# A two-layer recurrent kernel, second layer: gate products written straight to the token banks, scan carries copied by VectorE, a three-pass softplus, and a new order of jobs

## The reference

```python
xz = einsum('bld,ed->bel', xn, W_in);  x, z = split(xz, 2)         # 512 channels each
xc = silu(conv1d_causal(x, conv_w, K=4) + conv_b)
dt, Bm, Cm = split(einsum('bdl,ed->ble', xc, W_x), [128, 144])
delta = softplus(einsum('blr,dr->bdl', dt, W_dt) + b_dt)
state = exp(delta * A) * state + (delta * xc) * B_t                # 16 states a channel, a scan over time
y = sum over the states of C_t * state, + D * xc
y = y * silu(z)
s = einsum('bdl,ed->ble', y, W_out) + b_out
x = x + s * silu(xn @ binarized(weight).T + bias)
```

## Time and profile before

| | |
|---|---|
| median of 3 runs | 1458.35 us (1455.82 to 1458.52) |
| the profiled execution | 1456.31 us, of which the span 1454.5 us |
| busy over the span | PE 95%, DVE 71%, ACT 61%, POOL 62% |
| first scan of the second block to the last | 630.7 us to 1436.8 us |

### The profile page before, as it was taken

The page is one execution under the profiler, slowest core; times in us unless marked ns, Lnnn a source line. Parts: engine busy times, 40 slices in busy tenths (PEclk is TensorE's granted clock), DMA queues, the critical chain, the costliest instruction groups (busy, mean ns, idle before and its releaser), DMA issues.

```text
span 1454.5 us, 23554 instructions
## 1 busy us (share of the span) xinstructions
PE 1379.5 (95%) x8652; PEld 1076.8 (74%) x8652; DVE 1026.0 (71%) x1377; ACT 889.0 (61%) x1461; POOL 904.2 (62%) x578
## 2 busy tenths in 40 slices
PE   7999999999999999988899999999999999999887
PEld 4445469999999999456667767777767768768777
DVE  7755542332322323589899998999999998998996
ACT  4211121111111111399999989999999999999893
POOL 4222211232222222159989989989999989999995
PEclk9999999999999999989999999999999999999999
DMA  9921146766766764123342452533534443523532
GB/s 299 404 91 40 58 136 227 269 251 233 267 248 249 273 241 151 41 55 79 88 102 74 98 119 61 131 88 94 125 80 96 102 102 88 129 76 84 134 91 69
DMA packets 57761, 205.17 MB, mean 141 GB/s; under 512 B 6575, under 2 KB 32815, under 8 KB 48822
## 3 DMA queue, kind: packets, MB, share of 16 engines
q1 hardware_dynamic: 42358, 146.55, 28.9%
q0 software_dynamic: 15296, 57.19, 17.3%
HBM read 141.78 MB, written 31.00 MB: 119 GB/s over the span
## 4 chain that ended last, share of the span: by engine, by line
PE 49%; POOL 21%; DVE 10%; ACT 10%; issue 7%; DMA 3%; SPq 0%; POOLq 0%; DVEq 0%; ACTq 0%
PE bank L1518 17%; POOL hst L690 16%; PE bank L1531 8%; PE bank L1463 7%; DVE hst L1363 5%; ACT dA L883 4%; PE bank L1723 3%; PE bank L1703 3%; POOL dbuT L672 3%; ACT dbuT L872 2%; DMA hst<-hst 2%; PE bank L1585 2%; POOL xpad L650 1%; PE bank L1493 1%; PE bank L1592 1%
## 5 line engine op out<-in xcount | busy, mean ns | idle before, releaser
L1363 DVE TENSOR_TENSOR_SCAN hst<-dA,carry,bank 128x512 f32<-128x512 f32 x512 | 631.4, 1266 | 52.4 <-PE bank L1703 41.2
L690 POOL TENSOR_TENSOR hst<-hst,c_bc 128x2048 f32<-128x2048 f32 x127 | 581.8, 4592 | 20.9 <-DVE hst L1363 6.0
L1703 PEld LDWEIGHTS bank<-ident,dbuT 128*128 128x128 f32 x2048 | 241.7, 142 | 180.1 <-issue 93.0
L883 ACT ACTIVATE dA<-delta,negA 128x512 f32<-128x512 f32 x512 | 357.2, 714 | 5.9 <-DVE hst L1363 5.8
L1703 PE MATMUL bank<-ident,dbuT 128*128 128x128 f32 x2048 | 316.3, 278 | 41.0 <-DVE hst L1363 35.9
L872 ACT ACTIVATE dbuT<-duT,bT 128x512 f32<-128x512 f32 x382 | 271.8, 712 | 8.1 <-PE bank L1703 8.0
L1518 PEld LDWEIGHTS bank<-f_sb,w_gu 128*128 128x128 f32 x2240 | 255.5, 192 | 2.7 <-ACT f_sb L754 1.0
L1518 PE MATMUL bank<-f_sb,w_gu 128*128 128x128 f32 x2240 | 256.0, 275 | 0.7 <-ACT f_sb L754 0.7
L1723 PE MATMUL bank<-ident,hst 128*128 128x128 f32 x1520 | 215.7, 273 | 3.4 <-DMA hst<-hst 3.4
L625 POOL TENSOR_TENSOR x_sb<-x_sb,neg_half 128x1 f32<-128x1 f32 x35 | 23.0, 656 | 260.5 <-DVE x_sb L1180 260.5
L1723 PEld LDWEIGHTS bank<-ident,hst 128*128 128x128 f32 x1520 | 176.2, 142 | 4.2 <-DMA hst<-hst 4.1
(11 more groups left out here) (212 smaller groups left out, 1760.6 us busy)
## 6 DMA issues: line engine op xcount, KB each, us to landing
w_gu<-in_w_gu SPq DMA_DIRECT2D x35, 2048.0 KB, 7.3
c_bc<-c_rows SPq DMA_DIRECT2D x64, 512.0 KB, 4.2
hst<-hst POOLq DMA_DIRECT2D x31, 1024.0 KB, 9.1
sorted_x<-sg_a SPq DMA_DIRECT2D x12, 387.0 KB, 11.4
x_sb<-sorted_x SPq DMA_DIRECT2D x35, 129.0 KB, 7.2
x_sb<-in_x SPq DMA_DIRECT2D x8, 512.0 KB, 7.7
w_d<-in_w_d SPq DMA_DIRECT2D x1, 4096.0 KB, 21.3
x_mix<-x_sb SPq DMA_DIRECT2D x1, 4096.0 KB, 31.5
```

The costliest lines, as they stand in the source:

```text
L690: pool.tensor_tensor(h[:], h[:], c, ALU.mult).then_inc(hc_ready, 1)
L883: act.activation(dA[:, at % DA_BUFS, :], delta[q % B][:, d, :], ACT.Exp, scale=negA[:, d, n:n + 1]).then_inc(dA_ready, 1)
L1363: v.tensor_tensor_scan(h[:, d, :], dA[:, at % DA_BUFS, :], bank[4 + u % 2][:], carry1[q % B][:, n, d:d + 1], ALU.mult, ALU.add).then_inc(s ...
L1703: ins = pe.transpose(bank[4 + u % 2][:, i * P:(i + 1) * P], dbuT[(DS * q + n) % DBU_BUFS][:, i, d * P:(d + 1) * P], ident[:])
```

## The change

1. z: the products now run in the chunk that uses them, in units 9 to 14, and write to the token banks 0 to 3, each as soon as `gate_y` of the chunk before has read the bank. ScalarE applies silu while it reads the banks (four 128x512 instructions in unit 21), writes `zy`, and `add_skip` follows in units 18 and 19, waiting for that silu. VectorE's four copies are gone.
2. Carries: VectorE copies them (`keep_carry`), one 128x4 copy a state, after the first scan of the next state (`CARRY_AT`). GpSimd's multiply waits for that copy.
3. Softplus is max(v, ln(1 + exp(16) * exp(-max(16 - v, 0)))): three ScalarE passes, and one `scalar_tensor_tensor` on VectorE with the bias and the maximum.
4. The tables are rewritten: silu in units 21 and 22 rather than 24, two of GpSimd's four `dbuT` states moved (4, 7, 10, 11 to 4, 8, 9, 11), the sums given units one by one, du transposes and others some units earlier.

```diff
-POOL_SPREADS = (4, 7, 10, 11)
+POOL_SPREADS = (4, 8, 9, 11)
...
-                        pool.tensor_copy(carry1[q % B][:, n, :], h[:, :, CH - 1]).then_inc(carry_done, 1)
+                        pool.wait_ge(carry_done, g + 1)
                     pool.wait_ge(c_loaded[n // 2 % 2], 64 * q + 16 * (n // 4 + 1))
-                    if q < CHUNKS - B:
-                        pool.wait_ge(carry_done, g + 1)
...
-            def silu_z(t):
-                wait_freed(act, t - 1, "Z3")
-                act.activation(zy[t % B][:], zy[t % B][:], ACT.Silu).then_inc(z_ready, 1)
+            def silu_z(t, i):
+                act.wait_ge(z_made, TPC * t + i + 1)
+                act.activation(zy[t % B][:, i, :], bank[i][:], ACT.Silu).then_inc(z_ready, 1)
...
+            def below_cap(t, d):
+                wait_full(act, t, f"DL{d}")
+                act.activation(soft[:, d, :], place(t, f"DL{d}")[:], ACT.Relu, bias=cap_dt[:, d:d + 1],
+                               scale=-1.0).then_inc(soft_step, 1)
...
-                is_freed(v.tensor_tensor(delta[(t + 1) % B][:, d, :], place(t, f"DL{d}")[:], soft[:, d, :], ALU.add),
-                         t, f"DL{d}")
+                is_freed(v.scalar_tensor_tensor(delta[(t + 1) % B][:, d, :], place(t, f"DL{d}")[:],
+                                                cols1[:, d, KC + 1:KC + 2], soft[:, d, :], ALU.add, ALU.max), t, f"DL{d}")
...
+            def keep_carry(g):
+                q, n = divmod(g, DS)
+                v.wait_ge(scan_done, DB * g + DB)
+                v.tensor_copy(carry1[q % B][:, n, :], hst[g % STATE_BUFS][:, :, CH - 1]).then_inc(carry_done, 1)
...
-            def z_part(t, i, k):
-                M = claim(t, f"Z{i}") if k == 0 else place(t, f"Z{i}")
+            def z_part(q, i, k):
+                if k == 0:
+                    wait_past(pe, y_gated, TPC * (q - 1) + i + 1 if q else 0)
...
             def add_skip(q, i):
-                wait_past(pe, y_gated, TPC * (q - 1) + i + 1 if q else 0)
+                pe.wait_ge(z_ready, TPC * q + i + 1)
```

More of the change, by code:

```diff
@@ L54 @@
 AHEAD = 4
-POOL_SPREADS = (4, 7, 10, 11)
+POOL_SPREADS = (4, 8, 9, 11)
 SPREAD_LEAD = 4
[L57 to L60, removed]
+PE_X = (0, 1, 2, 3, 6, 8, 9, 10)
+PE_G = (14, 15, 16, 17)
+PE_DT = (21, 23, 24, 25)
+PE_DL = (28, 34, 37, 41)
 PE_BC = (29, 30, 31, 32)
[L62 to L75, removed]
+PE_BT = 45
+PE_DUT = (47, 48, 52, 56)
+PE_Z = (9, 9, 10, 11, 11, 12, 12, 14)
+PE_XN = (58, 61)
+PE_YF = (21, 32, 35, 37)
+PE_OUT = (39, 40, 41, 44, 46, 47, 49, 50)
+PE_SKIP = (18, 18, 19, 19)
+ACT_X = (3, 6, 12, 15)
+ACT_SILU = 21
+PIECES = 4
+ACT_SOFT = (34, 38, 43, 44)
+ACT_DUT = (50, 55, 56, 58)
+ACT_YF = (24, 36, 40, 42)
+DVE_CONV = (3, 4, 5, 6, 7, 9, 10, 11, 12, 13, 14, 15)
+DVE_GATE = (8, 9, 10, 12)
 DVE_DT = 27
-DVE_DELTA = (31, 36, 41, 44)
+DVE_DELTA = (31, 36, 40, 44)
 DVE_BC = 33
[L79 to L83, removed]
+DVE_BT = 46
+ACT_XN = (None, None)
+ACT_DT = None
+ACT_BC = None
+DVE_RESULT = (45, 51)
+DVE_XN = (62, 63)
+POOL_DU = (6, 8, 9, 11)
 POOL_RES = 13
@@ L127 @@
                 ADDED[q - back, n, d] = len(ADDED) + 1
+WHOLE = [max(at for (chunk, n, d), at in ADDED.items() if chunk == q) for q in range(CHUNKS)]
 CLAIMED = {"DT": PE_DT[0], "BC": PE_BC[0], "BT": PE_BT}
@@ L848, in slot @@
                         turn_du(q, ACT_DUT.index(u))
+                    if u == ACT_DT:
+                        dt_rows(q)
+                    if u == ACT_BC:
+                        bc(q)
+                if q + 2 < CHUNKS and u in ACT_XN:
+                    turn_xn2(q, ACT_XN.index(u))
                 if u == ACT_SILU:
+                    for i in range(TPC):
+                        silu_z(q, i)
                     for h in range(2):
                         silu_gate(q, h)
+                if u == ACT_SILU + 1:
                     if q + 1 < CHUNKS:
@@ L891, in _ @@
             act.preload_act_table_set("natural_log_exp_and_others")
[L893 to L917, removed]
+            below_cap(-1, 0)
+            below_cap(-1, 1)
+            exp_capped(0, 1)
+            below_cap(-1, 2)
+            exp_capped(1, 2)
+            ln_capped(0, 3)
+            below_cap(-1, 3)
+            exp_capped(2, 4)
+            ln_capped(1, 5)
+            exp_capped(3, 6)
+            ln_capped(2, 7)
+            ln_capped(3, 8)
             turn_du(-1, 0)
@@ L927, in _ @@
                 for u in range(UNITS):
-                    if q > 0 or u > 1:
+                    if (q > 0 or u > 1) and u != ACT_SILU + 1:
                         decay(q, u)
-                    if u + AHEAD < UNITS:
-                        if q > 0 or u + AHEAD >= TPC:
+                    if u == ACT_SILU:
+                        decay(q, u + 1)
+                    if u == ACT_SILU + 1:
+                        for piece in range(u + AHEAD, u + AHEAD + PIECES):
+                            spread_du(q, piece)
+                    elif u + AHEAD < UNITS:
+                        if (q > 0 or u + AHEAD >= TPC) and not ACT_SILU + 1 < u <= ACT_SILU + PIECES:
                             spread_du(q, u + AHEAD)
@@ L1312, in _ @@
                     conv(-1, d, part)
[L1313 to L1318, removed]
-                v.wait_ge(relu_ready, d + 1)
-                make_delta(-1, d)
             def first_piece(i):
@@ L1352, in _ @@
                 for u in range(UNITS):
+                    if u % DB == CARRY_AT and (q or u > DB) and DS * q + u // DB <= DS * (CHUNKS - B):
+                        keep_carry(DS * q + u // DB - 1)
                     n, d = divmod(u, DB)
@@ L1739, in _ @@
                     x_half(-1, d, k)
-            for i in range(2):
-                for k in range(KB):
-                    z_part(-1, i, k)
             for d in range(2):
@@ L1772, in _ @@
                         spread(q + 1, 0)
-                    if u in PE_SKIP:
-                        add_skip(q, PE_SKIP.index(u))
+                    for part in range(TPC * KB):
+                        if PE_Z[part] == u:
+                            z_part(q, *divmod(part, KB))
+                    for i in range(TPC):
+                        if PE_SKIP[i] == u:
+                            add_skip(q, i)
                     for back, n, d in (SUMS_AT if q + 1 < CHUNKS else SUMS_LAST)[u]:
```

99 lines of the change are left out of this document (47 added, 52 removed), and 5 rows, old and new, of the table SUM_AT.

## The result

The changed kernel takes 1479.23 us in the median (1478.51 to 1479.60) against 1458.43 for the one before: 1.0146 times as long, 95% interval 1.0133 to 1.0159. It is slower by 20.8 us. The forecast was 1449 and faster; the time is outside the range, 0.2 us above the upper end (1479) of the rival in which the carry copies wait for GpSimd.

The account below looks back on a forecast made before the run. The pair TensorE and VectorE was taken to set the time. Seven periods x -1.2 = -8.4, start-up -1.5 and last chunk +0.7 gave -9.2 us: 1449 as a median, range 1438 to 1470.

Parts of the forecast that it names:

- the rival in which the carry copies wait for GpSimd: VectorE's carry copies wait for GpSimd's running instruction, +2.8 to +5 us in six chunks: 1466 to 1479; chance 0.30.
- the carry copy: On VectorE, 16 small copies a chunk 0.07 us apart: 1.1 us, most of it where TensorE is the later one.
- The break-even: A mean wait of 0.10 us a carry copy (96 copies against 9.2 us) decides between gain and loss.
- GpSimd's multiply now starts one scan and its job later ... 0.: GpSimd's multiply starts 1.3 to 1.8 us later; 5 us a chunk comes back and sums come 13 units later: 0.
- So taking the copies off GpSimd is worth nothing by itself.: GpSimd is no second bound: chunk 6, without carry copies, still took 102.70 us, so removing them gains nothing.
- The stretches: Per chunk: units 48 to 63 -5.1, 0 to 15 +0.8, 16 to 23 +3.4 less 0.3, 24 to 47 0: -1.2 us.
- the 0.3 for TensorE's lead: Units 16 to 23: TensorE's lead of up to one unit from light units 12 to 15 takes off 0.3 us.
- Softplus: ScalarE drops one pass four times a chunk, 2.3 us, but VectorE's waits end with TensorE: 0.
- silu gap: From unit 21 to the second table load ScalarE makes no decay for 11 us: 0, up to 1.5 us a chunk.
- skip waiting for silu: In units 18 and 19 `add_skip` waits for silu, with later spreads queued behind it: cost 0, upper end 1 us.
- Start-up -1.5: Before the first scan, z products, copies and four VectorE maxima leave the chain: -1.5 us (-0.5 to -2.5).
- Last chunk +0.7 (0 to 3): Last chunk: 6.9 us of z products where TensorE had room, skip terms in pairs: +0.7 us (0 to 3).

Follow-up runs that it names:

- e9: The changed kernel, carry copies kept, without the DMA that adds state 8 into state 9 (TensorE sums state 8): 1473.99 us, 1.0119 of the kernel before.
- e6: e3 without the DMA that adds state 8 into state 9 (TensorE sums state 8): 1449.99 us, 0.9944 of the kernel before.
- e11: e6 with VectorE's carry as a tensor-scalar multiplication by 1 instead of a reduction: 1472.31 us, 1.0109 of the kernel before.
- e3: The changed kernel with VectorE's carry copy written as a reduction (maximum over an axis of one element): 1468.67 us, 1.0065 of the kernel before.
- e8: The kernel before with only the carry moved to VectorE, as a reduction: 1457.83 us, 1.0003 of the kernel before.
- e10: e1 without the DMA that adds state 8 into state 9: 1465.30 us, 1.0066 of the kernel before.
- e12: The kernel before with only the three-pass softplus and the three-input delta: 1459.12 us, 1.0008 of the kernel before.
- e7: e6 with, in chunk 6, no merge of state 12 into 13 either (TensorE sums state 12): 1449.84 us, 0.9942 of the kernel before.
- e1: The changed kernel with the carry copies back on GpSimd, ahead of its multiply: 1478.86 us, 1.0158 of the kernel before.

## Why the prediction was wrong

**"The other edits", the carry copy: "1.1 us, most of it where TensorE is the later one".** This step failed. The mechanism was named, as the rival with 0.30, on the strength of one row; the forecast took the other branch. The break-even had been put at 0.10 us of waiting a copy; they wait 0.535 - 0.141 = 0.39. With the merge of state 9 out of the way it is 0.464 - 0.141 = 0.32, 31 us over 96 copies, and costs 24.0 us of time (e9 against e6) (the other 7 are hidden); the rival's 2.8 to 5 us a chunk held (4.2 to 4.6 in chunks 2 to 5, e9 against e6), and so did its range, 1466 to 1479, for e9. What should have decided between the branches was in the earlier trace rows: a VectorE instruction with one SBUF input at double rate. The Trainium skill, page "SBUF — State Buffer", section "Who interferes with whom", says that copies and tensor-scalar instructions can be in a 2-port mode and that a reduction on trn2 cannot and never contends with GpSimd. The traces agree on all three forms, down to four elements a partition: 464 ns in the mean for the copy and for tensor-scalar (e9, e11), 142 for the reduction (e6), 56 of whose 96 lie inside a running GpSimd instruction.

**"GpSimd's multiply now starts one scan and its job later ... 0."** This step failed too, and it was in no rival: the merge has no term in the prediction at all. I looked at the sums that follow the multiply 13 units later, and not at the transfer between them: state 9's multiply, then the DMA, 9.8 to 11.4 us from its issue to the scan that needs the buffer. The late multiply, which the step does name, is not what costs: in e3 the issue is no later than before (15.6 us after unit 36's scan for 15.8). In the kernel before, the transfer landed at 909.74 + 9.29 = 919.03 and the scan ran at 919.49, with 0.5 us to spare, and the trace of before had the sign of it, in chunk 0:

```profile
714.16 2.45 DVE L1363 TENSOR_TENSOR_SCAN hst<-dA,carry,bank 128x512 f32<-128x512 f32 x2 [4.01 <-DMA hst<-hst]
```

That wait was there to be read. It costs 18.7 us once the copies are cheap, 5.2 beside them: the two costs cover each other, since a VectorE that waits gives GpSimd time. Each without the other is 24.0 and 18.7 us; together they are 1479.2 - 1450.0 = 29.2.

**"So taking the copies off GpSimd is worth nothing by itself."** True of the kernel before (e8), but the reason given was wrong: the interval from 1174.66 to 1277.36 begins in chunk 5, and twelve of GpSimd's carry copies lie in it; chunk 6 itself took 101.3 us, 1.1 less than the middle chunks. And it said nothing of a kernel whose pair is faster: there the carries on GpSimd cost 15 us (e10 against e6). GpSimd is not full even so: in e10 it is busy for 94 to 95 of 103.4 to 105.0 us in chunks 2 to 5, and what holds the scans is one late piece of its work, the merge of state 13.

**The stretches.** Right in the main. In e6 units 0 to 15 take 29.3 us (forecast 29.9), 16 to 23 13.3 (13.0: the 0.3 for TensorE's lead did not come), 24 to 47 36.2 (36.7); units 48 to 63 take 22.8, for the 21.4 of the kernel after, because TensorE has four sums more there. The sum, 101.2 a period, was 101.6: errors of 0.3 to 1.3 us, of which the largest comes with the four sums and the others partly cancel.

**Softplus, silu gap, skip waiting for silu: 0.** Softplus was 0 in the whole time (e12), 0.4 us less in units 24 to 47. In the trace after, no scan in the middle chunks waits for `dA`, and TensorE stands idle before no skip term. Those two were not tested by themselves.

**Start-up -1.5.** It was -1.7 in the profiled execution. The other versions of the changed kernel lie between -0.7 and -3.2, and the new softplus alone gives nothing (e12), so this is read from single executions.

**Last chunk +0.7 (0 to 3).** Mis-sized: +8.8 after, of which 4.4 go with the merge of state 9 (e9), and +3.9 in e6. Of that, 2.8 us are units 16 to 23, 12.5 us for 9.7: the skip terms moved out of units 9 to 12, where VectorE's own jobs hide them, to where nothing does, and there are no units 48 to 63 full of Z products to give it back. This I read from the starts alone.

**What stays open.** Whether the load of `x_ld` beside the merge is what makes it 2 us longer was not tested. Chunk 1 takes 103.8 us in e6, two more than the next, and that too is a merge: chunk 0 is short there, state 13's merge was issued at 725.38 and landed 8.8 us later, and the scan of unit 4 ran at 734.33, after a wait of 2.1 us.

The best of the versions is e6 (or e7, the same): 0.9944 of the kernel before. The forecast of 1449 is about what the change gives once the two steps that failed are repaired, in part by luck: of the 6.3 us between the two profiled executions 5.9 are in chunk 0, where a wait of 4.0 us for the merge went; chunks 2 to 5 gain 0.6 to 1.1 us each, not 1.2, and chunk 1 and the last chunk lose 1.2 and 3.9.

## What to carry to other kernels

Before a small SBUF-to-SBUF instruction moves to VectorE beside a busy GpSimd, look at its form: a copy or a tensor-scalar instruction can wait for the whole of what GpSimd runs, a reduction over an axis of one element took the same numbers in 0.14 us. When one engine is made faster, follow the others' work to its end, transfers and the reuse of buffers included, and search the trace for every wait, however rare, that ends with them: the one in chunk 0 of the kernel before was the next bound. And when undoing a suspect gives nothing back, read the new trace before clearing it: e1 and the changed kernel take the same time for two different reasons.

## What the runs showed of the hardware

A wait of TensorE costs more than its length. In e1 its clock falls from the upper level (2.4 GHz) to the lower (1.2 GHz) during the 4.0 us wait for the DMA. Windows of 4 us: the columns are busy us and instructions of PE, PEld, DVE, ACT, POOL, then the granted clock, the DMA share and GB/s:

```profile
920.00:924.00 4.00, 2.56 (x17) 1.93 (x15) 2.48 (x3) 4.00 (x7) 3.85 (x3) 1.00 1.10 255
924.00:928.00 4.00, 1.41 (x7) 1.42 (x8) 1.33 (x2) 1.95 (x4) 4.00 (x2) 0.65 0.39 80
928.00:932.00 4.00, 4.00 (x21) 3.84 (x19) 3.57 (x3) 3.05 (x5) 3.85 (x3) 0.50 0.37 131
932.00:936.00 4.00, 3.94 (x35) 3.70 (x35) 3.40 (x3) 1.28 (x3) 3.85 (x3) 1.00 0.00 0
```

Four transposes, 0.60 us in the rows before the wait, are 1.12 behind it. The same happens in each of e1's chunks 0 to 5. In e3 it is not the same each time: in chunk 2 the scan of unit 52 waits for 2.52 us and the clock stays up, in chunk 3 it waits for 2.60 and the clock falls. The windows behind the two waits:

```profile
924.00:928.00 4.00, 3.10 (x27) 2.67 (x26) 4.00 (x6) 3.11 (x6) 3.50 (x2) 1.00 0.34 131
...
1028.00:1032.00 4.00, 3.88 (x23) 3.48 (x22) 3.40 (x4) 2.37 (x4) 4.00 (x1) 0.62 0.14 52
```

Units 48 to 63 take 24.1 us in the first and 25.1 in the second. It falls in chunks 0, 1, 4 and 5 too. Of e3's six runs, the two with the highest mean granted clock (0.989 and 0.991) took 1463.8 and 1462.5 us, the four with 0.983 to 0.987 took 1468.2 to 1470.1. In e6 the clock stays at 1.00 from 631 to 1341 us.

A copy on VectorE that meets GpSimd is not let in between instructions that follow each other closely: the copy at 888.42 in the kernel after met the second of four `dbuT` pieces, each about 1.0 us long and overlapping the next by 0.3, and ended with the fourth.
